# Loading x and the context a second time, laid out turned, in place of turning them on TensorE

## The reference

```
x_q = w_qk y;  x_k = w_qk x;  x_v = w_v x + b_v            # y is ctx
energy[n, m] = sum_c x_q[c, n] x_k[c, m]                   # 512 x 512
attention = softmax(energy, over m); attention /= 1e-7 + its column sums
x2 = x + relu(w_t (x - x_v attention) + b_t)
q = x2 Wq + bq;  k, v = ctx Wk + bk, ctx Wv + bv           # 32 query heads, 8 key heads of 16
out = softmax(q k^T / 4 + mask) v Wo + bo
result = layernorm(out + x2) * gamma + beta
```

## Time and profile before

| what | value |
|---|---|
| median of 3 runs | 786.86 us (785.52 to 790.73) |
| span of the profiled execution, first to last instruction | 788.3 us |
| busy share: PE, PEld | 94%, 77% |
| busy share: DVE, POOL, ACT | 76%, 73%, 61% |
| DMA | 84.86 MB, mean 108 GB/s |
| TensorE clock granted, mean | 0.978 of full speed |

### The profile page before, as it was taken

How to read it: one execution, slowest core, us unless ns; L and a number is a source line. 1 busy time by engine, 2 the same in 40 slices (tenths; PEclk the granted TensorE clock), 3 DMA queues, 4 the chain that set the end, 5 groups by cost and what they waited for, 6 DMA issues and landing times.

```text
span 788.3 us, 17370 instructions
## 1 busy us (share of the span) xinstructions
PE 738.5 (94%) x5015; PEld 605.9 (77%) x5015; DVE 601.3 (76%) x1047; ACT 481.4 (61%) x1074; POOL 571.8 (73%) x754
## 2 busy tenths in 40 slices
PE   6798999989999999999999999999999999998773
PEld 5686877878788788878878788887878888785642
DVE  5874885958779696878969686887969687795747
ACT  5754749376574947657493866758485775748161
POOL 4885388676877968686896868688796868757054
PEclk9999999999999999999999999999999999999796
DMA  8333251523426152343516134352614334241511
GB/s 306 106 95 91 78 141 55 141 78 120 110 87 163 53 146 82 108 110 96 153 63 153 67 120 110 100 136 73 165 44 139 98 111 119 77 121 61 134 37 60
DMA packets 55755, 84.86 MB, mean 108 GB/s; under 512 B 9520, under 2 KB 29616, under 8 KB 55600
## 3 DMA queue, kind: packets, MB, share of 16 engines
q1 hardware_dynamic: 55008, 84.25, 37.1%
q10 hardware_dynamic: 720, 0.27, 0.2%
HBM read 24.72 MB, written 8.39 MB: 42 GB/s over the span
## 4 chain that ended last, share of the span: by engine, by line
PE 80%; DMA 8%; DVE 3%; issue 3%; POOL 2%; SPq 2%; ACT 1%; DVEq 0%; POOLq 0%; ACTq 0%
PE banks L821 9%; PE banks L914 8%; PE banks L927 7%; DMA qstack<-mrep 5%; PE banks L861 4%; PE banks L939 4%; PE banks L885 4%; PE banks L862 4%; PE banks L863 4%; PE banks L941 3%; PE banks L940 3%; PE banks L808 3%; PE banks L806 3%; PE banks L807 3%; PE banks L794 3%
## 5 line engine op out<-in xcount | busy, mean ns | idle before, releaser
L1564 DVE TENSOR_REDUCE maxima<-banks 128x4 f32<-128x512 f32 x256 | 160.0, 685 | 9.9 <-PE banks L885 8.0
L1220 ACT ACTIVATE prob<-banks 128x512 f32<-128x512 f32 x256 | 134.9, 609 | 37.5 <-PE banks L914 36.4
L576 POOL TENSOR_TENSOR ta<-ta,cb_s 128x516 f32<-128x516 f32 x64 | 77.0, 1203 | 96.5 <-ACT ta L1161 96.5
L1589 DVE RECIPROCAL dens<-dens 128x512 f32<-128x512 f32 x30 | 100.5, 3348 | 50.9 <-DMA dens<-sides 50.9
L821 PE MATMUL banks<-ta,att 128*128 128x130 f32 x1024 | 120.2, 275 | 0.4 <-POOL ta L583 0.4
L821 PEld LDWEIGHTS banks<-ta,att 128*128 128x128 f32 x1024 | 117.9, 190 | 2.5 <-POOL ta L583 0.6
L1153 ACT ACTIVATE att<-banks,negmax 128x512 f32<-128x512 f32 x128 | 88.6, 714 | 21.1 <-DVE negmax L1514 20.8
L1514 DVE TENSOR_REDUCE negmax<-banks 128x1 f32<-128x512 f32 x128 | 85.8, 687 | 12.1 <-PE banks L808 11.9
L1204 ACT ACTIVATE qh<-banks,bq_s 128x256 fp32r<-128x256 f32 x64 | 30.7, 480 | 99.5 <-PE banks L863 99.5
L914 PE MATMUL banks<-qstack,kstack 128*128 128x512 f32 x256 | 80.7, 420 | 10.0 <-DMA qstack<-mrep 9.8
L861 PE MATMUL banks<-x2h,wq_h 128*128 128x256 f32 x256 | 74.6, 292 | 4.1 <-POOL x2l L644 4.1
(11 more groups left out here) (177 smaller groups left out, 1997.7 us busy)
## 6 DMA issues: line engine op xcount, KB each, us to landing
qstack<-qh SPq DMA_DIRECT2D x128, 128.0 KB, 2.3
xs<-in_x SPq DMA_DIRECT2D x16, 512.0 KB, 3.6
ys<-in_ctx SPq DMA_DIRECT2D x16, 512.0 KB, 3.6
kstack<-kph SPq DMA_DIRECT2D x128, 64.0 KB, 2.0
qstack<-ql SPq DMA_DIRECT2D x64, 128.0 KB, 2.3
out_x<-late SPq DMA_DIRECT2D x32, 256.0 KB, 2.1
dens<-sides SPq DMA_DIRECT2D x62, 128.0 KB, 2.0
kstack<-kpl SPq DMA_DIRECT2D x64, 64.0 KB, 2.0
```

Source lines behind the costliest of these rows:

```text
L1220: nc.scalar.activation(prob[:, 2 * p + odd], banks[:, slot(plan, f"st{j}{kv}")], exp_f).then_inc(sem["prob_done"], 1)
L1564: nc.vector.tensor_reduce(maxima[:, 0, :, p, :, g].rearrange("x o j -> x j o"), banks[:, slot(plan, f"mx{g}{p}")].rearrange("x (j o s) -> ...
L1589: nc.vector.reciprocal(dens[:], dens[:]).then_inc(sem["dinv_done"], 1)
```

## The change

The host also lays out x and ctx turned (`in_x_turned`, `in_ctx_turned`: pair, partition, column block, entry, token) and w_t transposed. SP loads them with a DMA of 512 KB each in a body: `xt` at the head of the body, `et` after `stack_maxima`. `cw` loses its identity columns (386 to 258, in all three matmuls), `ctx_transpose` goes, `ctx_high` and `ctx_low` become one instruction each of 1024 columns that reads `et` in SBUF, and x2 adds `xt`. The two bank places of et0 and et1 are left empty ("skip"). On PE `max_spread` comes ahead of `z_project(i, 0)` and the last energy; on DVE `max_split` comes ahead of `residual_add` and `row_statistics` of entry 1, and `max_rows` behind `energy_max(i, 1, 1)`.

```diff
-X0 = A0 + P
-CW = X0 + P
+CW = A0 + P
...
-    ("mx32", 2), ("mx33", 2), ("wo1", 3), ("et0", 1), ("et1", 1), ("en11", 1), ("en12", 1), ("z0", 0),
-    ("en13", 1), ("m", 2), ("b00", 1), ("b01", 1), ("st00", 2), ("st01", 2), ("st02", 2), ("st03", 2),
+    ("mx32", 2), ("mx33", 2), ("wo1", 3), ("skip", 1), ("skip", 1), ("en11", 1), ("en12", 1), ("m", 2),
+    ("z0", 0), ("en13", 1), ("b00", 1), ("b01", 1), ("st00", 2), ("st01", 2), ("st02", 2), ("st03", 2),
...
+            def load_xt(pair):
+                sp.dma_start(xt[:], xT[bass.ts(pair, 1)].rearrange("o p k j c -> p (o k) j c")).then_inc(xt_in, 16)
+
+            def load_et(pair):
+                sp.dma_start(et[:], ctxT[bass.ts(pair, 1)].rearrange("o p k j c -> p (o k) j c")).then_inc(et_in, 16)
...
             def next_y(i):
                 wait(sp, "y_split", i, 1)
-                wait(sp, "et_ps", i, 1)
                 load_y(i + 1)
+
+            def next_et(i):
+                wait(sp, "etl_done", i, 0)
+                load_et(i + 1)
+
+            def this_xt(i):
+                wait(sp, "x2_done", i - 1, 1)
+                load_xt(i)
...
                 q = i - 1
+                if s1:
+                    this_xt(i)
                 if load_next:
                     next_x(i)
...
                 if s2:
                     stack_maxima(q)
+                if load_next:
+                    next_et(i)
+                if s2:
                     gather_denominators(q, 0)
...
             load_y(0)
+            load_et(0)
...
+            load_xt(0)
             first_iteration(0, True, True, False, False, setup=True)
...
-                mm(o[:, 0:X0], a, cw_l[:, 0:X0], start=False, stop=True).then_inc(sem["tva_ps"], 1)
+                mm(o[:, 0:CW], a, cw_l[:], start=False, stop=True).then_inc(sem["tva_ps"], 1)
...
                 if s1:
-                    ctx_transpose(i, plan, 0)
-                    ctx_transpose(i, plan, 1)
                     energy(i, plan, 1, 1)
                     energy(i, plan, 1, 2)
+                if s2:
+                    max_spread(q, plan, i)
                 if s0:
                     z_project(i, plan, 0)
                 if s1:
                     energy(i, plan, 1, 3)
-                if s2:
-                    max_spread(q, plan, i)
...
-                nc.scalar.activation(eth[:, :, j], banks[:, slot(plan, f"et{j}")].rearrange("p (k s) -> p k s", k=KC),
-                                     copy_f).then_inc(sem["eth_done"], 1)
+                nc.scalar.activation(eth[:], et[:], copy_f).then_inc(sem["eth_done"], 1)
...
+                dve.wait_ge(xt_in, i * 16 + 16)
+                stt(x2[:, :, j], ta[:, j, :, A0:CW], 0.0, xt[:, :, j], ALU.max, ALU.add
...
+                tt(etl[:], et[:], eth[:].bitcast(F32), ALU.subtract).then_inc(sem["etl_done"], 1)
...
+                    score_max(q, plan, 3, 3)
+                    max_split(q)
                 if s3:
                     residual_add(i - 2, plan, 1)
-                if s2:
-                    score_max(q, plan, 3, 3)
-                if s3:
                     row_statistics(i - 2, 1)
-                if s2:
-                    max_split(q)
-                if s1:
-                    ctx_low(i, plan, 0)
+                if s1:
+                    energy_max(i, plan, 1, 1)
                 if s2:
                     max_rows(q, plan)
-                if s1:
-                    energy_max(i, plan, 1, 1)
                 if s3:
                     root_guess(i - 2)
                 if s1:
                     energy_max(i, plan, 1, 2)
                     energy_max(i, plan, 1, 3)
-                    ctx_low(i, plan, 1)
+                    ctx_low(i)
                 if s0:
                     z_low(i, plan, 0)
```

More of the change, by code:

```diff
@@ L111, in ring @@
         if stage in stages:
+            if name == "skip":
+                at = (at + 1) % slots
+                continue
             bank = first + at
@@ L116, in ring, with build_xattn @@
     return plan, (at, held)
-def build_xattn(nc, x, ctx, mask, w_qk, w_v, w_t, b_t, Wq, Wk, Wv, Wo, bo, gamma, beta, columns, consts, out):
+def build_xattn(nc, x, ctx, xT, ctxT, mask, w_qk, w_v, w_tT, b_t, Wq, Wk, Wv, Wo, bo, gamma, beta, columns, consts, out):
     es = ExitStack()
@@ L149, in build_xattn @@
         cw_s = setup[:, 4 * N:4 * N + CW]
-        wqk_s, wv_s, wt_s, wtT_s = (setup[:, 5 * N + n * P:5 * N + (n + 1) * P] for n in range(4))
+        wqk_s, wv_s = (setup[:, 5 * N + n * P:5 * N + (n + 1) * P] for n in range(2))
+        wtT_s = cw_s[:, A0:CW]
         late = sb("late", [P, 2, 2, N])
@@ L171, in build_xattn @@
         ys = sb("ys", [P, 2, N])
+        xt = sb("xt", [P, KC, 2, P])
+        et = sb("et", [P, KC, 2, P])
         mk = sb("mk", [P, 2, P])
@@ L208, in build_xattn @@
         dens = sb("dens", [P, G * P])
+        flag_row = dens[0:1, 0:2 * P]
         stage_o = prob[:, 0:G]
@@ L574, in add_bias @@
                 wait(pool, "ta_raw", i, 4 * j + 2 * h + 1)
-                part = ta[:, j, 2 * h:2 * h + 2, 0:X0]
-                nc.gpsimd.tensor_tensor(part, part, cb_s[:].unsqueeze(1).broadcast_to([P, 2, X0]), ALU.add
+                part = ta[:, j, 2 * h:2 * h + 2]
+                nc.gpsimd.tensor_tensor(part, part, cb_s[:].unsqueeze(1).broadcast_to([P, 2, CW]), ALU.add
                                         ).then_inc(sem["ta_done"], 1)
@@ L772, in _ @@
             mm(banks[:, GRAM_BANK, 0:P], wqk_s, wqk_s, start=True, stop=True).then_inc(gram_ps, 1)
-            pe.wait_ge(cst_in, 16)
-            pe.wait_ge(wt_in, 16)
-            nc.tensor.transpose(banks[:, SETUP_BANK, 0:P], wt_s, ident).then_inc(wt_ps, 1)
             def z_project(i, plan, j):
@@ L822, in attend @@
                 last.then_inc(sem["b_ps"], 1)
-            def ctx_transpose(i, plan, j):
-                name = f"et{j}"
-                if j == 0:
-                    pe.wait_ge(y_in, i * 16 + 16)
-                wait_slot(pe, plan, name, i)
-                for k in range(KC):
-                    last = nc.tensor.transpose(banks[:, slot(plan, name), bass.ts(k, P)], ys[:, j, bass.ts(k, P)], ident)
-                last.then_inc(sem["et_ps"], 1)
             def kv_project(i, plan, name, n, done):
@@ L835, in kv_project @@
                     pe.wait_ge(wkv_ready, 1)
-                wait(pe, "etl_done", i, 1)
-                wait_slot(pe, plan, name, i, have=("etl_done", 0, 1))
+                wait(pe, "etl_done", i, 0)
+                wait_slot(pe, plan, name, i)
                 o = banks[:, slot(plan, name), 0:2 * P]
@@ L1162, in tva_raw, with ctx_high @@
                                      ).then_inc(sem["ta_raw"], 1)
-            def ctx_high(i, plan, j):
-                wait(act, "et_ps", i, j)
+            def ctx_high(i):
+                act.wait_ge(et_in, i * 16 + 16)
                 wait(act, "q_ps", i - 1, 3)
-                nc.scalar.activation(eth[:, :, j], banks[:, slot(plan, f"et{j}")].rearrange("p (k s) -> p k s", k=KC),
-                                     copy_f).then_inc(sem["eth_done"], 1)
+                nc.scalar.activation(eth[:], et[:], copy_f).then_inc(sem["eth_done"], 1)
             def k_high(i, plan):
@@ L1296, in iteration @@
                     tva_raw(i, plan, 1, 3)
-                    ctx_high(i, plan, 0)
-                    ctx_high(i, plan, 1)
+                    ctx_high(i)
                 if s0:
@@ L1424, in _ @@
             act.dma_start(cst[:], consts).then_inc(cst_in, 16)
-            act.dma_start(wt_s, w_t).then_inc(wt_in, 16)
+            act.dma_start(wtT_s, w_tT).then_inc(wt_in, 16)
             for dst, src in ((wv_s, w_v), (cols[:], columns), (cb_s[:, A0:A0 + P], b_t.partition_broadcast(P))):
```

44 lines of the change are left out of this document (17 added, 27 removed), and 2 rows, old and new, of the table FIRST_WIDE_USES.

## The result

The changed kernel takes **782.53 us** (median of 10 runs, 780.33 to 784.82) against 788.22 us (785.31 to 790.73) of the kernel before in the same comparison: ratio 0.9922, 95% interval 0.9901 to 0.9943. The forecast was 780 us, with 774 to 796 as the range. The profiled execution spans 780.3 us in place of 788.3. The run of that profile took 782.72 us; in the thirteen profiled runs with a time on record it is 1.9 to 2.9 us above the span. So the profiled execution of the kernel before was one of its longer ones, some 2 us above the median: the spans differ by 8.0 us, the medians by 5.7, and 7.0 had been forecast.

The account below looks back on a forecast made before the run. Bound: TensorE, but ahead of the scores the maxima's DMA, landing behind the context load. Bodies 1 to 14 gain 8.4 us, body 15 gains 1.1, the fill loses 2.5: 7.0 us less, forecast 780 us, range 774 to 796.

Parts of the forecast that it names:

- What bounds the body: Ahead of the scores: the maxima land behind the 512 KB context load, 4.28 us after its issue, not by their own issue.
- own landing: Rival at the scores: maxima land by their own 3.34 us, a body gains at most 0.85 us, 776 us; chance 0.17.
- full TensorE gain: Rival on TensorE: it gets all it saves, 2.1 us a body, giving 758 us; chance 0.06.
- How much earlier q's last part is: In the projection: six narrowed units ahead save 0.70 us, less 0.1, so q's last part and the scores come 0.6 earlier.
- the term of 0.1 us for mx1's bank: On TensorE: mx1's fourth matmul waits some 0.2 us for VectorE to reduce mx03; half of that was taken off.
- K's projection has more: Behind the scores: the z bank has 0.35 us to spare before st04 needs it, and k's projection has more.
- the upper bound of 2.5 us: ctx_low on VectorE slowed by POOL's SBUF reads: 1.3 us taken, 2.5 at most; as a rival 793 us, chance 0.16.
- Moving `max_spread` and `max_split` forward lets the issue come earlier: On TensorE and VectorE: the maxima's DMA can be issued earlier, but its landing still follows q's last part.
- The steady bodies: Bodies 1 to 14 were forecast to gain 0.6 us each, 8.4 us together.
- The fill, 2.5 us lost: Before the loop: et and xt, 1.05 MB ahead of the x load, cost 2.5 us, bounds 1.3 and 3.4.

Follow-up runs that it names:

- first_later_spread: Changed kernel with the maxima's DMA ahead of the context load, the root's guess behind the last two energy maxima, and max_spread behind z_project: 0.9753 of the kernel before.
- all_edits: first_later_spread plus the first xt issued behind the next x in the fill: 0.9744 of the kernel before, 769.19 us.
- columns_only: Kernel before with only the identity columns removed and x turned by the host; context transposes and old order of the maxima stay: 1.0003.
- after_old_order: The whole change with the maxima's split and spread left in their old place on TensorE, VectorE and in the banks: 0.9984 of the kernel before.

## Why the prediction was right, and where only its sum was

- **What bounds the body: right.** The maxima land by the issue of the context load and not by their own. From that issue to the scores it was 4.53 us before and 4.51 after, and 4.56 to 4.71 in the four kernels that took away or moved one part, with the issue of the maxima 0.57 to 1.48 us behind it. The landings in the traces say the same (means over the bodies 4 to 13): 4.28 to 4.48 us behind the context load in all eight kernels that issue it first, 2.82 to 3.91 behind their own issue. In body 15, with no context load ahead, they took 2.48 us (chain of waits):

```profile
698.99 2.48 DMA qstack<-mrep
```

  With the queue's order turned they land 2.56 to 2.62 us behind their own issue in six kernels, and in the steady bodies the wait is gone from four of these (first_later_spread and all_edits keep 0.2 us). The rivals "own landing" and "full TensorE gain" fall with that.
- **How much earlier q's last part is: right in kind, mis-sized, the term of 0.1 us for mx1's bank.** `mx1` lost 0.3 (0.81 against 0.51), and columns_only gives 0.38 for all of it where 0.6 were forecast. In the changed kernel the fourth matmul of mx1 begins at 281.80, 0.3 us behind the third and as soon as VectorE has reduced mx03 (281.75); the prediction had 0.2 for that wait and counted half of it.
- **"K's projection has more" to spare: this step failed.** The second half of the scores waits behind `k_low`, and that behind the addition of x. That half begins 6.56 us behind the first on the mean in the changed kernel and 6.75 in the old order, against 6.45 at the shortest: 0.1 and 0.3 us a body. I had weighed VectorE against GpSimd at `ctx_low` only, where the upper bound of 2.5 us was not reached (1.22). The Trainium skill (SBUF — State Buffer, Who interferes with whom) says that the one that issued first keeps the shared access for the whole instruction, and the other stands still. That holds for both directions here: GpSimd's 1.05 us beside `ctx_low`, and VectorE's end 0.55 us behind GpSimd's in both timelines. In the bodies 4 to 13 of all fourteen kernels every addition longer than 0.70 us had begun beside a GpSimd step, and it ended 0.54 to 0.56 us behind it.
- **"Moving `max_spread` and `max_split` forward lets the issue come earlier": wrong, and harmless.** With `max_rows` behind an energy maximum the new order issues later behind the context load than the old one: 1.48 us in place of 0.96 alone, and 0.72 in place of 0.57 with the rest of the change. The landing didn't follow it, as the same sentence says. Alone the new order is worth nothing (0.9992). With the rest it moves GpSimd's split against the addition, and without it the change has no measurable gain.
- **The steady bodies**: 0.34 us instead of 0.6, from these two terms (0.38 less 0.12, and 0.08 back between the stack and the scores).
- **The fill, 2.5 us lost: one half of it failed, the other isn't seen in the time.** Between the two profiles the load of x landed 0.2 us later, but it also moves by itself: with the loads ahead of it as before it landed at 17.90, 18.57 and 19.41 (three kernels), with `et` alone ahead of it at 17.87 to 18.80 (three), with `xt` alone or both at 19.63 to 20.14 (eight). So `xt` costs some 1.3 us, the price of one load, and `et` nothing that shows. The loads issued behind x probably took a part of the delay (321 in place of 174 GB/s from 20 to 25 us); why `et` cost nothing is open. And the first scores don't show the 1.3: with the fill as before they came at 67.20 to 68.63, in the changed kernel at 67.29.
- **Bodies 1 and 2**, 1.97 us, weren't in the sum as bodies of their own. The wait for the maxima is 0.4 to 3.3 us long from body 1 to body 3 in these two profiles, at other places in each, and one stop in each is followed by the lower clock. That the 1.97 us come from the change is not shown.

So 780 was met partly by luck: the sum had 2.6 us too much in the ten steady bodies, and the 2.5 us that it took off for the fill aren't seen; up to the first scores the profiles have 1.34 gained instead, which profiles of an unchanged fill have as well.

## What to carry to other kernels

Before taking work off the busiest engine, look at what lands last and what is queued ahead of it: exchanging two issues on SP's queue gave 0.987 where all that the change took from TensorE gave 0.992, and the two together with a VectorE step out of the way of a wait 0.976. In the steady bodies the exchange alone was worth less than the change (0.23 and 0.34 us); the rest of its gain came from the first bodies. When an instruction of VectorE with both inputs in SBUF stands ahead of a bank that TensorE needs, look which GpSimd step it meets; an edit elsewhere can move that meeting, so an ordering that is worth nothing by itself can decide whether another edit pays. Sum the first bodies apart from the steady ones, and compare several executions or kernels before giving a cause for a difference there.

## What the runs showed of the hardware

- The maxima's 64 KB took 2.48 us with no load ahead, 3.64 issued 0.73 us behind a load of 512 KB on the same queue; issued 0.57 to 1.48 us behind it they landed 4.28 to 4.48 us behind the large load's issue (means of eight kernels).
- An addition of 512 columns with both inputs in SBUF took 0.69 to 1.79 us, by what GpSimd was doing; where it was held it ended 0.55 us behind the GpSimd instruction that it met.
- After stops of 2.60 us (before), 3.30 (after) and 2.07 (after_old_order) TensorE's next five scores took 2.47 us in place of 1.40; after stops of 2.31 (before) and 3.23 (after_old_order, below) they took 1.40. The length of the stop alone didn't decide it.

```profile
117.24 1.40 PE L924 MATMUL banks<-qstack,kstack 128*128 128x512 f32 x5 [3.23 <-DMA qstack<-mrep]
```
